# Two 64-wide heads in one step: scores from the halves of TensorE's rows, and a fixed order of the engines around each pair

## What is computed

```
q = layernorm(x) @ Wq          # 8 x 256 x 1024, 16 heads of 64
k, v = split(ctx @ Wkv)
attn = softmax(mask(q @ k.T * scale))        # 256 x 256 for each head
out = (attn @ v) @ Wo          # layer 3: one more "null" key and value, and a layernorm of out
x = x + out
```

## Time and profile before

| | |
|---|---|
| median of 3 runs | 1907.28 us (1906.17 to 1908.28) |
| the profiled execution, its own time | 1906.62 us |
| its span, first to last instruction | 1904.9 us |
| busy: PE, DVE, ACT, POOL | 1628.0, 1193.0, 907.4, 295.9 us |
| mean granted TensorE clock | 0.942 of 2.4 GHz |

### The profile page before, as it was taken

The page is one execution under the profiler, slowest core; times in us unless marked ns, Lnnn a source line. Parts: engine busy times, 40 slices in busy tenths (PEclk is TensorE's granted clock), DMA queues, the critical chain, the costliest instruction groups (busy, mean ns, idle before and its releaser), DMA issues.

```text
span 1904.9 us, 38869 instructions
## 1 busy us (share of the span) xinstructions
PE 1628.0 (85%) x13373; PEld 1246.2 (65%) x13373; DVE 1193.0 (63%) x3066; ACT 907.4 (48%) x1990; POOL 295.9 (16%) x443
## 2 busy tenths in 40 slices
PE   4999999989997799996274479999958999999987
PEld 3788888876665588884163255666636777777765
DVE  5966666676666578885211364555447777877771
ACT  1566666663442467775052233333305655655552
POOL 3000000001100323321301532000010011011111
PEclk9999999999998899998587689999969999999999
DMA  9100000000000300000011020000000000000000
GB/s 263 50 1 0 0 0 0 0 2 1 1 0 0 92 1 0 0 1 1 26 44 28 11 52 1 1 1 0 0 0 1 1 0 0 0 0 0 0 1 23
DMA packets 32089, 28.87 MB, mean 15 GB/s; under 512 B 6058, under 2 KB 26419, under 8 KB 31812
## 3 DMA queue, kind: packets, MB, share of 16 engines
q1 hardware_dynamic: 30980, 25.66, 4.7%
q0 software_dynamic: 1024, 2.10, 0.4%
HBM read 21.52 MB, written 6.23 MB: 15 GB/s over the span
## 4 chain that ended last, share of the span: by engine, by line
PE 58%; DVE 19%; issue 10%; ACT 8%; POOL 3%; DMA 1%; SPq 1%; ACTq 0%; DVEq 0%; POOLq 0%
PE bank L1333 49%; PE bank L1337 9%; DVE PTs L2056 2%; DVE negm L2047 2%; DVE negm L2052 2%; ACT Pm L1194 2%; DVE Qz L2326 2%; ACT VxF L1151 1%; ACT PTs L1150 1%; ACT Pm L1294 1%; DVE Qz L1851 1%; ACT Pm L1258 1%; DVE VxF L678 1%; DVE st L1859 1%; POOL yn L922 1%
## 5 line engine op out<-in xcount | busy, mean ns | idle before, releaser
L1333 PE MATMUL bank<-kT,Qz 128*128 128x256 f32 (+1 forms) x1568 | 443.0, 388 | 4.0 <-issue 1.6
L1194 ACT ACTIVATE Pm<-bank,negm 128x256 f32<-128x256 f32 x784 | 326.7, 468 | 206.2 <-DVE negm L2052 203.7
L1333 PEld LDWEIGHTS bank<-kT,Qz 128*128 128x128 f32 x1568 | 249.4, 192 | 68.2 <-issue 16.9
L1337 PE MATMUL bank<-ident,Pm 128*128 128x128 f32 x1568 | 239.4, 276 | 48.9 <-DVE PTs L2056 40.3
L2056 DVE TENSOR_TENSOR PTs<-bank,PTs 128x512 f16<-128x512 f32 x384 | 261.9, 682 | 7.7 <-ACT PTs L1150 7.2
L1337 PEld LDWEIGHTS bank<-ident,Pm 128*128 128x128 f32 x1568 | 187.4, 141 | 112.0 <-issue 59.5
L1333 PE MATMUL bank<-xHL,R 128*128 (+3 forms) x1008 | 234.8, 381 | 13.6 <-DVE Qz L2326 13.5
L2052 DVE TENSOR_REDUCE negm<-bank 128x2 f32<-128x512 f32 x264 | 181.6, 688 | 95.2 <-PE bank L1333 91.3
L1150 ACT ACTIVATE PTs<-bank 128x512 f16<-128x512 f32 (+1 forms) x388 | 231.3, 596 | 3.1 <-PE bank L1337 3.1
L1294 ACT ACTIVATE Pm<-bank,upback 128x512 f32<-128x512 f32 x168 | 115.3, 686 | 198.8 <-PE bank L1333 198.5
L1333 PE MATMUL bank<-VxF,PTs 128*128 128x65 f16 (+3 forms) x4672 | 202.5, 187 | 3.0 <-DVE PTs L2056 2.8
(11 more groups left out here) (268 smaller groups left out, 2052.2 us busy)
## 6 DMA issues: line engine op xcount, KB each, us to landing
token_rows_by_expert<-wpad SPq DMA_DIRECT2D x10, 256.0 KB, 3.9
R<-in_L_ffn_ew SPq DMA_DIRECT2D x2, 1024.0 KB, 7.0
R<-in_L_ffn_w SPq DMA_DIRECT2D x1, 2048.0 KB, 10.0
R<-in_L_xattn_Wkv SPq DMA_DIRECT2D x2, 768.0 KB, 6.9
Qz<-token_rows_by_expert SPq DMA_DIRECT2D x23, 64.0 KB, 1.9
expert_rows<-Qz SPq DMA_DIRECT2D x23, 64.0 KB, 1.5
R<-in_L_ffn_w SPq DMA_DIRECT2D x1, 1408.0 KB, 12.9
R<-in_L_xattn_Wq SPq DMA_DIRECT2D x2, 512.0 KB, 3.8
```

The costliest lines, as they stand in the source:

```text
L1194: last = act.activation(Pm[:, k % 4, qt * S:(qt + 1) * S], bank[k % 2][:, qt * S:(qt + 1) * S], ACT.Exp, bias=negm[:, k % 4, qt:qt + 1])
L1333: return pe.matmul(o, l, r, start=start, stop=stop)
L1337: return pe.transpose(o, i, ident[0:n, 0:n])
```

## The change

For the 64-wide heads `scores` becomes `pair`: the masks of two heads are written with one product of 512 columns each, into banks 0 and 1, and the four score products use only the 64 rows of their head, in the order head a, head b, head a, head b. `Qz` holds 8 slots without zeros, the q evacuation is one move, and POOL's two zeroings go. The order of a batch is now written for eight pairs, here called periods 0 to 7: transposes and low halves of the pair before, `pair`, both softmaxes, in layer 3 `null` (difference and exponential of the null key for both heads), all fills, and at the end the value products and the norm of the pair before; in period 0 the fills stand behind these. The product with Wo is made in two steps, `woa` and `wo`, in one bank. The splits of layer 0's last batch are steps of their own, two at the end of each period from 1 on.

```diff
-WIDE = {1: [("k", 3)], 2: [("outT", -2)], 3: [("v", 1)], 4: [("q", 3)], 5: [("v", 3), ("outT", -1)],
-        7: [("wo", 0), ("resid", 0), ("q", 0), ("k", 0)], 8: [("outT", 0)], 9: [("q", 1)],
-        10: [("k", 1)], 11: [("v", 0)], 12: [("outT", 1), ("v", 2)], 13: [("q", 2), ("ln", 0)],
-        14: [("k", 2)]}
-WIDE_NULL = {0: [("q", 3)], 1: [("k", 3)], 2: [("outT", -2)], 3: [("v", 1)], 4: [("outN", 0), ("v", 3)],
-             5: [("outT", -1)], 7: [("wo", 0), ("resid", 0), ("turns", 0), ("q", 0), ("k", 0)],
-             8: [("outT", 0)], 9: [("q", 1)], 11: [("v", 0), ("k", 1)],
-             12: [("v", 2), ("outT", 1), ("resid2", 0)], 13: [("q", 2), ("sn", 0)], 14: [("k", 2)],
-             15: [("ln", 0), ("snt", 0)]}
+WIDE = {0: ([], [("v", 1), ("q", 3)]), 1: ([("outT", -1)], [("k", 3)]),
+        2: ([("woa", 0)], [("wo", 0), ("resid", 0)]), 3: ([("outT", 0)], [("v", 3)]),
+        4: ([("q", 0)], [("ln", 0), ("k", 0)]), 5: ([("q", 1), ("outT", 1)], [("v", 0)]),
+        6: ([("k", 1)], [("v", 2)]), 7: ([("outT", 2), ("q", 2)], [("k", 2)])}
+WIDE_NULL = {0: ([], [("v", 1), ("k", 3)]), 1: ([("outT", -1), ("outN", 0)], [("q", 3), ("turns", 0)]),
+             2: ([("woa", 0)], [("wo", 0), ("resid", 0)]), 3: ([("outT", 0)], [("v", 3)]),
+             4: ([("q", 0)], [("k", 0), ("resid2", 0)]), 5: ([("outT", 1)], [("v", 0), ("q", 1)]),
+             6: ([("k", 1), ("q", 2)], [("v", 2), ("sn", 0)]), 7: ([("outT", 2), ("ln", 0)], [("snt", 0), ("k", 2)])}
 NARROW = {4: [("outT", -1)], 7: [("wo", 0), ("resid", 0)], 13: [("ln", 0), ("turns", 0)]}
-PREVIOUS = [("outT", -2), ("outT", -1), ("outN", 0), ("wo", 0), ("resid", 0), ("resid2", 0), ("ln", 0)]
+PREVIOUS = [("outT", -2), ("outT", -1), ("outN", 0), ("woa", 0), ("wo", 0), ("resid", 0), ("resid2", 0), ("ln", 0)]
 OWN = [("q", 3), ("k", 3), ("v", 1), ("v", 3)]
+def pair_steps(p, fills_a, fills_b):
+    a, b = 2 * p, 2 * p + 1
+    st = [("turn", a - 2), ("turn", b - 2), ("low", a - 2), ("low", b - 2)]
+    if p < 8:
+        st += [("pair", a), ("softmax", a), ("softmax", b), ("null", p)]
+    st += fills_a
+    st += [("av", a - 2), ("av", b - 2), ("norm", p - 1)]
+    return st + fills_b
...
-    table = WIDE_NULL if A.null else WIDE if A.pieces >= 8 else NARROW
+    def kept(step):
+        if step in PREVIOUS:
+            return not first
+        return step in OWN or step[0] in ("outT", "turns") or not last
     st = []
+    if A.dh == 64:
+        for p in range(8):
+            fills_a, fills_b = [[step for step in part if kept(step)] for part in (WIDE_NULL if A.null else WIDE)[p]]
+            st += [(kind, k) for kind, k in pair_steps(p, [], []) if k >= 0 or not first][:-3 if p or not first else None]
+            late = fills_b if p == 0 else []
+            st += fills_a + (fills_b if p else [])
+            if p or not first:
+                st += pair_steps(p, [], [])[-3:]
+            st += late
+            if last and A.n == 0 and 1 <= p:
+                st += [("split", i) for i in range(2 * p - 2, min(2 * p, UP_BLOCKS[0]))]
+        return st
...
-        for step in table.get(i, []):
-            if step in PREVIOUS:
-                if not first:
-                    st.append(step)
-            elif step in OWN or step[0] in ("outT", "turns") or not last:
-                st.append(step)
+        st += [step for step in NARROW.get(i, []) if kept(step)]
...
-    return [("q", 0), ("q", 1), ("q", 2)] + ([("sn", 0), ("snt", 0)] if A.null else []) + [("turns", 0)]
+    return [("q", 0), ("q", 1), ("q", 2)] + ([("sn", 0), ("snt", 0), ("turns", 0)] if A.null else [])
...
+    if A.dh == 64:
+        st = [(kind, k - 16 if kind != "norm" else k - 8) for kind, k in pair_steps(8, [], [])]
+        return st + [("outT", -1), ("outN" if A.null else "turns", 0), ("woa", 0), ("wo", 0), ("resid", 0)] + (
+            [("resid2", 0)] if A.null else [])
...
-                Q4 = Qz[:, :, :].rearrange("p (g u) s -> p g u s", u=2)
-                v = src[:, :].rearrange("p (g s) -> p g s", s=S)
-                move(Q4[0:64, 2 * k:2 * k + 2, 0, :], v[0:64], A.scale)
-                return move(Q4[64:128, 2 * k:2 * k + 2, 1, :], v[64:128], A.scale)
+                return move(Qz[:, 2 * k:2 * k + 2, :].rearrange("p h s -> p (h s)"), src[:, :], A.scale)
...
-            pool.memset(Qz[:, :, :], 0.0)
...
-                            if A.null:
-                                act.activation(pn[:, :, k], dn[:, k % 4, :], ACT.Exp)
...
+                        elif kind == "null" and A.null:
+                            need(act, s.dn, b * 8 + (k + 1))
+                            at = (2 * k) % 4
+                            act.activation(pn[:, :, 2 * k:2 * k + 2].rearrange("p q h -> p h q"),
+                                           dn[:, at:at + 2, :], ACT.Exp)
+                        elif kind == "split":
+                            t, lo, _ = UP[A.n]
+                            if k == 0:
+                                act.wait_ge(up_scale, A.n + 1)
+                            else:
+                                act.wait_ge(up_low, blocks_before(A.n) + k)
+                            move(block_parts(A.n, k)[0], cols(t, lo + 512 * (k + 1), 512),
+                                 upscale[:, A.n:A.n + 1]).then_inc(up_high, 1)
...
-                    elif kind == "wo":
-                        fills_read(b, m)
-                        for qt in range(2):
+                    elif kind in ("woa", "wo"):
+                        if kind == "woa" or A.dh != 64:
+                            fills_read(b, m)
+                        for qt in range(2) if A.dh != 64 else (0,) if kind == "woa" else (1,):
...
+                        if kind == "pair":
+                            if k == 0 and kinds == "first":
+                                fills_read(b, m)
+                            need(pe, s.exp, b * nh + k)
+                            for u in range(2):
+                                o = bank[u][:, :].rearrange("p (q s) -> p q s", s=S)
+                                if A.mask == "full":
+                                    mm(o, identb[:, :], mb0[:, :, :], True, False)
+                                else:
+                                    mm(o, onesb[:, :], mb3[:, bass.ts(b, S)].unsqueeze(1).to_broadcast([P, 2, S]),
+                                       True, False)
+                            for qt in range(2):
+                                for u in range(2):
+                                    rows = slice(64 * u, 64 * u + 64)
+                                    last = mm(bank[u][:, qt * S:(qt + 1) * S],
+                                              Qz[rows, k // 2, qt * P:(qt + 1) * P], kT[rows, k // 2, :],
+                                              False, qt == 1)
+                                    if qt == 1:
+                                        last.then_inc(s.scores.sem, 1)
+                        elif kind == "scores":
...
-                                if A.mask == "full":
-                                    mm(o, identb[:, :], mb0[:, qt, :], True, False)
-                                elif A.mask == "key":
-                                    mm(o, onesb[:, :], mb3[:, bass.ts(b, S)], True, False)
-                                last = mm(o, Qz[:, k, qt * P:(qt + 1) * P], keys_of(A, b, k), A.mask is None, True)
+                                last = mm(o, Qz[:, k, qt * P:(qt + 1) * P], keys_of(A, b, k))
...
-                                chain(dve.tensor_tensor(nm, nm, nsn[:, :, k], ALU.min))
-                                dve.tensor_tensor(dn[:, k % 4, :], nm, nsn[:, :, k],
-                                                  ALU.subtract).then_inc(s.negmax.sem, 1)
+                                dve.tensor_tensor(nm, nm, nsn[:, :, k], ALU.min).then_inc(s.negmax.sem, 1)
...
+                        elif kind == "split":
+                            t, lo, _ = UP[A.n]
+                            high, low = block_parts(A.n, k)
+                            dve.wait_ge(up_high, blocks_before(A.n) + k + 1)
+                            dve.scalar_tensor_tensor(low, cols(t, lo + 512 * (k + 1), 512),
+                                                     upscale[:, A.n:A.n + 1], high,
+                                                     ALU.mult, ALU.subtract).then_inc(up_low, 1)
```

34 lines of the change are left out of this document (19 added, 15 removed).

## The result

The changed kernel takes 1980.25 us (1974.05 to 1985.94, four runs), the kernel before, run beside it, 1907.78 (1906.17 to 1910.34). The ratio is 1.0381, 95% interval 1.0361 to 1.04: **slower by 72 us**. Slower was forecast, but by 16 us, and the time lies above the range.

The account below looks back on a forecast made before the run. PE was taken to bound layer 0, with an ACT and DVE chain close behind; third-fill waits (+1.7 us a batch in layer 0, +0.4 in layer 3) and smaller terms summed to +16.5, so 1923 us, range 1911 to 1942.

Parts of the forecast that it names:

- What bounds the kernel: Attention: PE alone in layer 0, busy 47.23 of 47.66 us a batch; in layer 3 an ACT and DVE chain at hand.
- The third fill of period 4: Layer 0: k0 waits until ACT, behind both softmaxes, copies q0 out of its bank; period 8.7 us, PE idle some 3.4.
- The clock falls: PE's clock drops after stalls, up to 2 us in half the layer 0 batches, as much in layer 3; 1940 to 1955, chance 0.06.
- The price of the overlap: A pair's four score products: eight passes in five slots of 0.21, 1.07 us, against 0.87 full overlap or 1.74 none.
- rival 2: Score products: little or no overlap, 1971 us; or half way, a drain at row changes, 1947; chance of either 0.18.
- rival 4: Score products overlap in full, all else as forecast: 1 us a batch less, 1907; within 0.2% of no change, chance 0.10.
- Rival 2's other half: PE drains between 128-row and 64-row products: 0.17 twice a pair, 1.5 us a batch, 1947 us; either half 0.18.
- PE's own work in a batch of layer 0: Masks stay at 0.43 and scores take 1.07 a pair, so PE's work falls by 0.67 a pair, 5.4 us a batch.
- Layer 3: Its eight periods sum to 54.0 us, 54.4 with restarts, +0.4 a batch; six middle batches +2.5.
- The first batches: Layer 0's first batch +1 for block maxima ahead of DVE's maxima; layer 3's first and last together +1.
- PE stays the bound: The hand chain is too long in stalled periods, so part of the 0.67 a pair comes through: 1860 to 1903, chance 0.28.

Follow-up runs that it names:

- warm: The changed kernel with dummy bfloat16 products on PE ahead of each fill that waits for the evacuation of its period's first fill; 1945.57 us, ratio 1.021.
- mid_same_rows: av_mid with both heads of a pair reading rows 0 to 63, so their score products cannot lie beside each other; 1950.43 us, ratio 1.0243.
- av_mid: The changed kernel with the value products and the norm between the two lists of fills of a period; 1898.44 us, ratio 0.9963.
- mid_ln_late: av_mid with layer 0's step ln in period 6 instead of period 4; 1897.94 us, ratio 0.9961.
- mid_some: The changed kernel with value products between the fill lists only in periods 4, 5, 7 (layer 0) and 1, 5, 6, 7 (layer 3); 1920.21 us, ratio 1.0074.

## Why the prediction missed

Where the extra time of the profiled executions lies, in us against the kernel before. The intervals are those between POOL's context copies; the last row is all that is outside the others, where the copy stands at another place of its batch than before, so that first intervals grow and the end shrinks (by 9.4 us).

| stretch | before | forecast | after | `warm` |
|---|---|---|---|---|
| layer 0, third interval (yn) | 47.66 | +1.7 | +6.3 | +9.6 |
| layer 0, the four next | 190.60 | +6.8 | +21.0 | +7.3 |
| layer 3, second interval | 54.19 | +0.4 | +7.3 | +5.5 |
| layer 3, the four next | 216.07 | +1.6 | +19.3 | +5.3 |
| the rest | 1396.4 | +6 | +13.5 | +10.4 |
| span | 1904.9 | +16.5 | +67.4 | +38.1 |

1. **What bounds the kernel** was right in the main: PE in layer 0, with a chain through ACT and DVE close behind. In `warm`, with the clock taken out, all eight periods of layer 0 come within 0.3 us of their forecasts, and the batch is at 49.49 where 49.4 was forecast (restarts included). The third fill of period 4 was to start 7 us after the period's first transpose and starts 7.1 after it (332.70 against 325.62). The stall there is 2.92 us where 3.4 was forecast, and PE waits 5.6 us a batch and not some 8, because more of the batch is work (4 below).
2. **The failed step: "The clock falls", chance 0.06, 1940 to 1955.** This is rival 3. It was seen as a mechanism, with its place, and even with its price of 2 us for a stall, but it was given to half of the batches only, and left out of the sum, so the forecast has the stall and then gives the work behind it at full clock. Measured: waits of 2 to 3 us come twice in every batch, and of the steady batches of both layers none has a clock of 1.00 (0.90 to 0.97 in those shown); 35 us by `warm`, of the 57 between forecast and result. The other 22 are mostly in items 5 and 6: by the table 8 us in the third interval of layer 0, 9 in layer 3, 5 elsewhere. The evidence called on against the fall was the row with waits up to 1.2 us, which could not speak for stalls of 3. The trace of the kernel before had rows that could, between the two layers that are changed: after a single wait of 2.05 us a group that took 1.11 just ahead of it (682.94) takes 2.05.

```profile
686.09 0.63 PE L1337 MATMUL bank<-ident,Pm 128*128 128x128 f32 x4 [2.05 <-DVE PTs L2056]
686.96 2.05 PE L1333 MATMUL bank<-kT,Qz 128*128 x4
```

3. **The price of the overlap** came out in size, 1.06 to 1.07 us for 1.07, but by luck. The forecast had five steps of 0.21, the second pass of one product beside the first of the next. Measured are four steps, with both heads' passes side by side, and 0.1 us lost at each end. So no overlap (rival 2) is refuted, and the full overlap of rival 4 is there, without its 0.87. Rival 2's other half, a drain at each change between 128 and 64 rows, 0.34 a pair on top of the 1.07, is there in part: the two changes cost 0.4 a pair, of which 0.2 lie within the 1.07. That one after the other costs 1.74 left these out: 1.92 (`mid_same_rows`). For the packing the Trainium skill ("TensorE: Matmul & The Clock Gate", on packing small matmuls) has a factor of 3.07 with four row groups; with two row groups and two passes a product it is 1.92 / 1.07 = 1.8 here, and 2 by the steps alone. The rule of the Trainium skill ("TensorEngine Tiling (Array Packing)", key properties) that a change of tiling mode drains the engine gives no price; the traces agree with a loss of 0.20 at each change, and whether it is a drain or the weights that are not loaded ahead, no run here tells apart.
4. **A smaller term was missed**: PE's own work in a batch of layer 0 falls by 3.4 us (47.23 to 43.80 in `av_mid`), not by the 5.4 forecast. These changes are the step: the forecast kept the masks at 0.43 a pair and the first fill behind the scores at 0.87, and they take 0.53 and 0.97 (328.43 to 329.40), 1.6 us a batch. The last 0.4 is not traced.
5. **Layer 3** came out at 55.3 at full clock for 54.4: periods 3 and 6 are 0.4 to 0.5 longer, 1 is 0.3 longer, 5 is 0.4 shorter. Four intervals of it make 4 us.
6. **The first batches** were put at +1 each, and both meet a late POOL. In layer 0 the third interval holds a wait of 5.8 us for POOL's yn, which the change had moved forward with `ln` (period 4 for head 13 of 16). The step that is moved was costed on PE alone; POOL starts on that batch's norm at 120.65 us in the changed kernel and at 121.85 in the kernel before: it was always late there, and `ln` now asks for it earlier. `mid_ln_late` shows that the wait goes (5.0 us) when `ln` stands late. The second interval of layer 3, +5.5 even in `warm`, has the same in another place: `resid2` was moved from head 12 to period 4 (heads 8 and 9), and DVE, and PE behind it, stand for POOL's normed rows:

```profile
1555.05 0.43 DVE L2195 TENSOR_TENSOR xnew<-R,x 128x256 f32<-128x256 f32 x1 [3.44 <-POOL R L1063]
```

   In both, POOL begins 6.9 or 7.0 us after the end of its context copy, and 0.33 after it in the batch that follows; the profile shows nothing that it waits for. What delays it stays open, and no run moved `resid2` back.

The rival "PE stays the bound" (0.28) was wrong for this order. Its times are reached one step away from it: with value products between the fills the kernel is at 1898, and with one fill between the softmaxes at 1884, inside that rival's 1860 to 1903, though PE still waits there, 2.7 and 1.2 us in a steady batch of layer 0.

## What to carry to other kernels

Work moved off the bound engine pays only where its next instruction is ready: before taking products away from it, see what lies between the first fill and the third, and put the products that need nothing (here the value products of the pair before) there, not behind. And where a forecast holds a single stall on TensorE of the size seen here (1.6 to 2.9 us), price it twice, once as a wait and once as the work behind it at half clock; dummy products into a bank that is overwritten anyway tell the two apart in one run. A period should be judged together with its neighbours: changing only the three or four periods that stall recovered less than changing all eight. A step that a reordering moves forward has to be checked on the engine that feeds it, in the first batch too.

## What was new about the chip

- Score products of fp32 on rows 0 to 63 and 64 to 127, issued in turn, start together and take a step of 0.21 or 0.22 us a pass, as one product does on the same 64 rows and on full rows: eight passes are four steps on two sets of rows and eight on one (1.07 and 1.92 us with what is lost at the ends).
- A change between products of 128 and of 64 rows costs about 0.20 us each way here, half ahead of the first pass and half behind it; the load of the weights is not ahead of the products there.
- The granted clock went to its lower level, 1.2 GHz, behind single waits of 2.92 us (`after`), 1.97 (`mid_some`) and 1.61 (`av_mid`). The length of the wait does not settle it: behind the 2.92 at 281.66 it stayed at 1.00, and in `av_mid` it stayed there in three batches with the same 1.61 or 1.62. In the period shown the work from 332.70 to 338.61 took up to twice its time.
